# Weighing two units behind the masking in the attention stage of a graph network kernel

## What is computed

```python
h = x @ W
s_src = h @ a[:D_OUT, 0]
s_dst = h @ a[D_OUT:, 0]
e = s_src[row] + s_dst[col]
e = jnp.where(e > 0, e, ALPHA * e)
row_max = jax.ops.segment_max(e, row, num_segments=n)
e_exp = jnp.exp(e - row_max[row])
row_sum = jnp.maximum(jax.ops.segment_sum(e_exp, row, num_segments=n), EPS)
att = e_exp / row_sum[row]
h_prime = jax.ops.segment_sum(att[:, None] * h[col], row, num_segments=n)
return jax.nn.elu(h_prime)
```

## Time and profile before

| | us |
|---|---|
| median of 3 runs | 2517.28 (2516.28 to 2518.36) |
| profiled execution | 2518.34 |
| its span in the trace | 2516.4 |
| attention stage, from first masking | about 267 of it |
| busy: TensorE / VectorE / ScalarE | 2242.5 / 1080.8 / 906.5 |

### The profile page before, as it was taken

The page is one execution under the profiler, slowest core; times in us unless marked ns, Lnnn a source line. Parts: engine busy times, 40 slices in busy tenths (PEclk is TensorE's granted clock), DMA queues, the critical chain, the costliest instruction groups (busy, mean ns, idle before and its releaser), DMA issues.

```text
span 2516.4 us, 31022 instructions
## 1 busy us (share of the span) xinstructions
PE 2242.5 (89%) x9795; PEld 1242.6 (49%) x9796; DVE 1080.8 (43%) x3021; ACT 906.5 (36%) x1867; POOL 628.4 (25%) x426
## 2 busy tenths in 40 slices
PE   4777776989885999689899999999999999998998
PEld 3444444855553554434444554455545644454444
DVE  5488886999995445623212121122112211112302
ACT  2698887878874233312111111111111111012200
POOL 1000001510001443133344434443444334420000
PEclk9888887589998999889999999999999999999999
DMA  5477773111222111133312232223222321214583
GB/s 164 162 217 209 214 211 98 0 42 50 64 67 68 1 1 30 46 83 61 90 21 33 47 70 45 29 44 68 38 41 33 60 56 21 30 38 160 215 305 104
DMA packets 186163, 209.75 MB, mean 83 GB/s; under 512 B 102413, under 2 KB 163455, under 8 KB 181980
## 3 DMA queue, kind: packets, MB, share of 16 engines
q1 hardware_dynamic: 116074, 157.51, 20.6%
q0 software_dynamic: 56720, 1.28, 6.7%
q10 hardware_dynamic: 13260, 49.53, 5.5%
HBM read 125.44 MB, written 82.84 MB: 83 GB/s over the span
## 4 chain that ended last, share of the span: by engine, by line
PE 52%; DMA 3%; DVE 1%; issue 0%; ACT 0%; DVEq 0%; ACTq 0%
PE banks L1603 24%; PE banks L1628 20%; PE banks L1725 5%; DMA feat<-hnD 3%; PE banks L1681 1%; PE banks L1589 1%; DMA out_dram<-big 1%; PE banks L1690 0%; DVE HN L1896 0%; DVE banks L1891 0%; ACT banks L1788 0%; DVE HN L1893 0%; PE banks L1706 0%; DVE big L1942 0%; DVE big L1940 0%
## 5 line engine op out<-in xcount | busy, mean ns | idle before, releaser
L804 POOL DMA_INDIRECT WT<-lists x391 | 614.4, 1571 | 870.8 <-DMA WT<-lists 856.3
L1603 PE MATMUL banks<-big,feat 125*128 125x500 f16 (+1 forms) x3150 | 607.1, 353 | 19.8 <-DMA feat<-hnD 15.4
L1603 PEld LDWEIGHTS banks<-big,feat 125*128 125x128 f16 x3150 | 306.6, 97 | 310.5 <-DMA feat<-hnD 16.2
L1628 PE MATMUL banks<-H,U 128*128 128x500 f32 (+1 forms) x756 | 302.8, 541 | 9.4 <-issue 9.4
L1628 PE MATMUL banks<-aT,V 128*128 128x500 f32 (+1 forms) x756 | 296.4, 538 | 3.4 <-DVE HN L1896 3.4
L761 PE MATMUL banks<-wide,ohs 128*125 128x500 f16 x628 | 187.7, 441 | 39.3 <-DVE wide L682 23.9
L1628 PEld LDWEIGHTS banks<-aT,V 128*128 128x128 f32 x756 | 143.1, 190 | 145.5 <-issue 97.5
L1628 PEld LDWEIGHTS banks<-H,U 128*128 128x128 f32 x756 | 142.6, 191 | 139.1 <-issue 101.7
L1884 DVE SCALAR_TENSOR_TENSOR HN<-banks,bh,HN 128x500 f32<-128x500 f32 (+1 forms) x70 | 47.8, 683 | 378.3 <-ACT HN L1786 354.4
L1786 ACT ACTIVATE HN<-banks,bs 128x500 f32<-128x500 f32 (+1 forms) x70 | 44.3, 632 | 381.1 <-PE banks L1628 381.1
L682 DVE TENSOR_SCALAR wide<-pairs,wcol 128x500 f16<-128x500 f16 x628 | 176.1, 344 | 0.0
(11 more groups left out here) (252 smaller groups left out, 2441.5 us busy)
## 6 DMA issues: line engine op xcount, KB each, us to landing
big<-WT ACTq DMA_DIRECT2D x25, 1562.5 KB, 7.4
WT<-zero SPq DMA_DIRECT2D x39, 980.0 KB, 6.7
wide<-keyD SPq DMA_DIRECT2D x80, 320.0 KB, 4.0
hTD<-HN SPq DMA_DIRECT2D x40, 250.0 KB
hnD<-stg SPq DMA_DIRECT2D x32, 250.0 KB
feat<-hnD SPq DMA_DIRECT2D x4, 2000.0 KB
H<-hTD SPq DMA_DIRECT2D x16, 500.0 KB
work<-xhD SPq DMA_DIRECT2D x28, 250.0 KB
```

The lines of the kernel that those rows point to most:

```text
L804: nc.gpsimd.indirect_dma_start(out=WT, out_offset=bass.IndirectOffsetOnAxis(ap=lists[:, 0, t - first:t - first + 1], axis=0), in_=lists[:, ...
L1603: last = nc.tensor.matmul(SUMS[s % 2][half][:, 0:wid(ch)], rows_, A[:, j, cols(ch)], start=(j == 0 and part == 0), stop=(j == T - 1 and pa ...
L1628: last = nc.tensor.matmul(PS[bank][:, 0:w], wt_[:, kt, g:g + 128], v[:, kt, 0:w], start=(n == 0), stop=(n == len(terms) - 1))
```

## The change

VectorE's program in the attention now weighs the unit two behind the one that it has just masked, instead of the one behind it. After the loop the last two units are left to weigh instead of one. The programs of the other engines are as before, ScalarE's late copies among them.

```diff
+BEHIND = 2
...
                 for s, (ch, g) in enumerate(steps):
                     for q in range(rows[ch]):
                         logit(s, q)
-                        if u:
-                            weigh(u - 1)
+                        if u >= BEHIND:
+                            weigh(u - BEHIND)
                         u += 1
...
-                weigh(u - 1)
+                for v in range(u - BEHIND, u):
+                    weigh(v)
                 share(SC - 1)
```

## The result

The changed kernel takes 2534.90 us as the median of 4 runs (2531.27 to 2540.40), the kernel before 2517.82 (four runs, one more than in the table ahead of the prediction). The ratio is 1.0071 with a 95% interval of 1.0052 to 1.0090, so it is slower by 13 to 23 us. Forecast were 2537.3 us and +20.

What follows compares the result with a forecast made beforehand. A two-slot ring between VectorE's masking and weighing and TensorE's transposes was taken as the floor under the step time; its growth summed to 20.9 us, less 1.0 for the exponential, net +20 on 2517.3: 2537.3 us, range 2525 to 2552.

Steps and rivals of the forecast that it cites:

- step 3, blocks 1 to 3: Four-tile steps with the product with W before the transposes: 5.69 us now, 6.74 by the ring, 3.2 us in all.
- step 6, blocks 1 and 3: Steps of 5.79 us at clock 0.55, already waiting for transposes: each grows by 0.99, 2.0 us in all.
- step 0, blocks 4 to 6: Three-tile steps going from 3.81 to 4.37 us: twice 0.56, 1.1 in all, block 4's being already longer.
- step 6, blocks 4 and 5, and the tail: Steps of 4.55 us at clock 0.75 with VectorE waiting, and the stage's tail: 0.99 more each, 3.0 us.
- everything else: The weighing's wait for ScalarE's exponential, 0.8 us in the table, taken as 1.0 us gained.
- The ring's links: First masking, previous step's last weighing, its transposes, first masking two steps on; grows by 1.25 or 0.99 us per step.
- I leave the four falls as they are: Clock falls in step 6 of blocks 1, 3, 4 and 5 stay; one more or less is about 1.8 us.
- the last two come from the same ring: Of three listed waits: masking for transposes (9.8 us) and weighing for the exponential (0.8 us) share one ring.
- The covers: ScalarE's late copies cost nothing (up to 0.3 us a step if uncovered); steps 4 and 5 don't grow.
- The exponential was the real limit: Rival: distance two frees VectorE from waiting on ScalarE; -8 us with every clock fall gone, 2509; 5%.
- The clock swings: Rival: TensorE's new short pauses bring clock falls in three-tile blocks too, +20 us on top, 2557; 8%.
- The ring is hidden: Rival: slack swallows the ring and only the ten places where VectorE already waits grow, 0 to +5 us, 2520; 12%.

Runs made afterwards that it cites:

- with idle work: Kernel before and changed kernel, TensorE transposing the identity ahead of its wait for the weighing (steps 4 and 5, blocks 1 to 6): 2510.11 and 2530.50 us.
- with the ring kept short, weighing two behind: Against the kernel before, two behind inside a step, each step's last unit weighed as before: 2512.83 us; with TensorE also transposing the identity in pauses, 2509.72 us.
- With three behind: Weighing three units behind the masking instead of the changed kernel's two: 2583.33 us, ratio 1.0252 to the kernel before.

## Why the prediction was right

The mechanism, the place and the size held. By the steps of the sum, each measured as the difference of the step between two profiled executions: the changed kernel less the kernel before, and the same pair with idle work, where no clock falls:

| term | forecast | measured | with idle work |
|---|---|---|---|
| step 2, blocks 1 to 3 | 1.8 | 1.8 | 1.8 |
| step 3, blocks 1 to 3 | 3.2 | 2.4 | 2.4 |
| step 6, blocks 0 and 2 | 1.4 | 1.4 | 1.4 |
| step 6, blocks 1 and 3 | 2.0 | -2.3 | 1.4 |
| the rest of block 0 | 1.3 | 1.1 | 1.7 |
| step 0, blocks 4 to 6 | 1.1 | 1.3 | 2.3 |
| step 1, blocks 4 to 6 | 1.5 | 2.0 | 2.0 |
| step 2, blocks 4 to 6 | 3.0 | 3.4 | 3.4 |
| step 3, blocks 4 to 6 | 2.6 | 2.0 | 2.0 |
| step 6, blocks 4 and 5, and the tail | 3.0 | 4.6 | 1.7 |
| everything else | -1.0 | -0.4 | -0.5 |
| sum (before rounding) | 19.9 | 17.3 | 19.5 |

- **The ring's links were read rightly.** 5.61 us measured against 5.60, 4.97 against 4.86, 4.64 against 4.64 for step 6 of block 2 (629.30 to 633.94). Three-tile steps 1 and 2 came out 0.1 longer because TensorE now pauses ahead of each: its transposes take 2.21 us, where the ones I took, in a row without a pause ahead of it, had 2.10 and VectorE's release behind them.
- **Step 3 was sized too large.** I took 1.24 us for the product with W from a row in which it stood at the end of other products. Behind a pause it holds the transposes up for 0.98 us only, and in three-tile blocks 0.76 instead of 0.97.
- **The clock was the weak term.** "I leave the four falls as they are" was wrong in its parts. The changed kernel has four falls in the stage too, but at other places. Those of blocks 1 and 3 didn't come, so their step 6 shrank by 1.1 us each instead of growing by 1.0. One came in step 5 of block 3, which is 6.96 us long with it and without, and one at the tail, where it added 1.7. The first two rows are the changed kernel's, the third is its tail with idle work:

```profile
664.24:671.20 6.96, 4.94 (x18) 3.30 (x18) 6.61 (x26) 4.61 (x9) 0.00 (x0) 0.75 0.03 5
784.34:792.87 8.53, 6.41 (x27) 5.06 (x28) 4.60 (x17) 4.65 (x10) 0.00 (x0) 0.80 0.23 62
...
783.21:790.08 6.87, 6.49 (x43) 5.29 (x43) 4.60 (x17) 4.54 (x10) 0.00 (x0) 1.00 0.24 66
```

- **The closeness of the sum is in part luck.** With idle work 19.5 us stand against a forecast of 19.9, but by errors that cancel. I had added the ring's whole growth to steps 6 whose present length held a clock fall; without falls they grow by 0.7 and 0.5 us and not by 1.0. I had left out step 0 of block 4 as already longer. It was longer for a fall alone, and without one it grows by 1.1 us, 3.79 to 4.91. And "the last two come from the same ring" in the prediction is a slip: it holds for the first two of the three waits named there.
- **The covers held.** ScalarE's copies now wait 25 us and cost nothing. Steps 4 and 5 kept their length within 0.2 us in blocks 1 to 6 (step 5 of block 2 is 6.97 us against 7.13). Everything behind the stage is as long as before.
- **The rivals.** *The exponential was the real limit* is out: with the ring kept short, weighing two behind, as far as it was tried, gains 1.0 us of the stage. *The clock swings*: the many short pauses of the changed kernel, 0.3 to 1.5 us, left the clock at 1.00 in steps 1 to 3, in all windows shown above; the falls still stand behind pauses of 2.0 to 2.8 us. With three behind, where TensorE pauses 1.3 to 2.8 us in most steps, the clock fell in ten places, so this rival had the direction right for a longer ring. The section on queue cycling that the forecast cited, from the page TensorE: Matmul & The Clock Gate of the Trainium skill, has no case in the changed kernel's short pauses. *The ring is hidden* is out, with two slots the growth arrives step by step.

One thing is left open: whether a fall comes after a given pause. In the kernel before one of 2.79 us had a fall behind it and one of 2.80 had none, and no run here tells what decides it. The changed kernel's own runs spread over 9 us.

## What to carry to other kernels

Where one engine waits for a whole group of another's work and its release frees the slot that the other needs next, each place that the last member of the group moves back is added to every round that this ring bounds, while other members may move for nothing. Write such a ring down link by link from start-to-start times and compare it with the present round, since an engine's idle share says nothing about it.

## What the runs showed of the hardware

- Filling TensorE's pauses of 1.5 to 2.8 us with transposes of a constant kept the granted clock at 2.4 GHz in stretches where it had fallen to 1.2, and was worth 7.1 us of a stage of 263, 0.3% of the kernel (ratio 0.9969).
- Clock falls came and went in stages that the edit didn't touch, and moved the time behind the stage by up to 5 us between profiled executions (1741.7 against 1736.5 us). Differences below that need the stage's own windows, not the kernel's time.
- The transposes of one step took 2.85 us where TensorE had stood idle before them and 2.75 where they followed a matmul directly, 2.21 against 2.10 in three-tile blocks, at the same granted clock: about 0.1 us for a start from rest.
